# Rows of six experts exchanged by DMA, normalised on GpSimd and turned on VectorE instead of TensorE

## The reference

```python
x = x + layernorm(attn(layernorm(x)))   # gate g = sigmoid(x Wg^T + bg), scan h = (1-g) h + g x, out = h Wo^T + bo
x = x + layernorm(ffn(layernorm(x)))
# ffn: eid = argmax(softmax(xf @ router_w + router_b)); rank of the token among those of its expert
# valid = rank < C (320)
# expert: y = relu(buf[e] @ w1[e] + b1[e]) @ w2[e] + b2[e]     E = 8, D = 256, H = 1024, buf[e] is [320, 256]
# out = y of its expert where valid, otherwise relu(xf @ ow1 + ob1) @ ow2 + ob2
```

## Time and profile before

| | |
|---|---|
| median of 3 runs | 1139.37 us (1139.37 to 1139.41) |
| the profiled execution's own time | 1139.46 us |
| its span, first to last instruction | 1137.5 us |
| mean granted TensorE clock | 0.996 |
| PE, DVE, ACT, POOL busy share | 98%, 87%, 68%, 58% |
| steps of the experts | from about 990 us to the end |

### The profile page before, as it was taken

How to read it: one execution, slowest core, us unless ns; L and a number is a source line. 1 busy time by engine, 2 the same in 40 slices (tenths; PEclk the granted TensorE clock), 3 DMA queues, 4 the chain that set the end, 5 groups by cost and what they waited for, 6 DMA issues and landing times. The chain is left out here.

```text
span 1137.5 us, 24653 instructions
## 1 busy us (share of the span) xinstructions
PE 1118.9 (98%) x7341; PEld 996.5 (88%) x7341; DVE 989.5 (87%) x2795; ACT 772.7 (68%) x1433; POOL 661.6 (58%) x734
## 2 busy tenths in 40 slices
PE   8999999999999999999999999999999999999996
PEld 4788988888888898888888888898889988899996
DVE  6888899899999999998989898999999888688885
ACT  5366676667766667666677666677666776687882
POOL 3556666656666665666666666566666655324443
PEclk9999999999999999999999999999999999999998
DMA  8211043222222222222222222222222220435430
GB/s 259 68 48 57 20 126 80 72 76 56 74 74 74 74 74 73 69 72 70 72 53 72 73 57 72 60 71 74 74 74 74 55 93 20 128 126 175 159 126 31
DMA packets 186314, 92.46 MB, mean 81 GB/s; under 512 B 121403, under 2 KB 182509, under 8 KB 186148
## 3 DMA queue, kind: packets, MB, share of 16 engines
q1 hardware_dynamic: 179108, 86.65, 27.3%
q0 software_dynamic: 7168, 5.34, 1.6%
HBM read 53.82 MB, written 38.76 MB: 81 GB/s over the span
## 5 line engine op out<-in xcount | busy, mean ns | idle before, releaser
L691 ACT ACTIVATE hid<-psH,biasT 128x512 f32<-128x512 f32 (+1 forms) x312 | 202.7, 650 | 206.0 <-PE psH L1432 203.9
L1538 PE MATMUL psY<-W_hi,hid_hi 128*128 128x256 f32 x1168 | 336.1, 288 | 0.3 <-DVE hid_lo L1112 0.2
L1541 PE MATMUL psY<-W_hi,hid_lo 128*128 128x256 f32 x1168 | 330.5, 283 | 0.0
L1540 PE MATMUL psY<-W_lo,hid_hi 128*128 128x256 f32 x1168 | 330.3, 283 | 0.0
L1430 PE MATMUL psH<-xfT_hi,W_hi 128*128 128x512 f32 (+1 forms) x624 | 235.8, 378 | 0.3 <-ACT hid L691 0.2
L1112 DVE TENSOR_TENSOR hid_lo<-hid,hid_hi 128x512 fp32r<-128x512 f32 (+1 forms) x308 | 200.1, 661 | 40.3 <-ACT hid_hi L696 37.0
L1431 PE MATMUL psH<-xfT_lo,W_hi 128*128 128x512 f32 (+1 forms) x624 | 235.0, 377 | 0.0
L1432 PE MATMUL psH<-xfT_hi,W_lo 128*128 128x512 f32 (+1 forms) x624 | 232.6, 373 | 0.0
L1538 PEld LDWEIGHTS psY<-W_hi,hid_hi 128*128 128x128 f32 x1168 | 223.0, 191 | 9.2 <-issue 1.5
L1540 PEld LDWEIGHTS psY<-W_lo,hid_hi 128*128 128x128 f32 x1168 | 223.3, 191 | 6.0
L1541 PEld LDWEIGHTS psY<-W_hi,hid_lo 128*128 128x128 f32 x1168 | 223.1, 191 | 0.0
(11 more groups left out here) (179 smaller groups left out, 2167.5 us busy)
## 6 DMA issues: line engine op xcount, KB each, us to landing
xin<-L_attn_x SPq DMA_DIRECT2D x32, 512.0 KB, 3.5
stage<-L_ffn_w SPq DMA_DIRECT2D x16, 1024.0 KB, 5.5
out<-outt SPq DMA_DIRECT2D x31, 512.0 KB, 2.8
stage<-L_attn_x SPq DMA_DIRECT2D x26, 512.0 KB, 3.5
stage<-tok SPq DMA_DIRECT2D x416, 32.0 KB
xbuf<-zrow SPq DMA_DIRECT2D x1, 2590.0 KB, 16.8
xin<-xbuf SPq DMA_DIRECT2D x8, 259.0 KB, 5.3
stage<-L_ffn_ow SPq DMA_DIRECT2D x2, 1024.0 KB, 8.8
```

Source lines behind the costliest of these rows:

```text
L691: act.activation(hid[j % 2][:, at:n], psH[:, j % 2, at:n], ACT.Relu, bias=bias).then_inc(s_hid, 1)
L1538: pe.matmul(dst, hi, w[0][:, j, :], start=(j == 0 and (tail or t % 2 == 0)), stop=False, skip_group_check=True)
L1540: pe.matmul(dst, hi, w[1][:, j, :], start=False, stop=False, skip_group_check=True)
L1541: last = pe.matmul(dst, lo_, w[0][:, j, :], start=False, stop=(j == HC - 1), skip_group_check=True)
```

## The change

For experts 2 to 7 (`blocked`), the normalised and transposed rows come about in another way. SyncE loads the rows a second time from `xbuf` in DRAM, in twelve DMAs a step: for each quarter of the partitions, the 32x32 squares of each half of the features, exchanged so that a square's feature block selects the partitions and its token block the columns (`xblk`, in the buffer `keep`), and the two scalars of each token (`sblk`, in `ngx`). GpSimd multiplies and adds the scalars, two tensor_tensor for each, and VectorE turns each 32x32 square into `psT`. VectorE's `norm2` at j = 2 and TensorE's transposes go for these experts. The rows in `xe` are still loaded for the residual; GpSimd's copy of them waits for the load instead of for `tok2`.

```diff
+def blocked(e):
+    return not isinstance(e[0], int) or 2 <= 2 * e[0] + e[1] < E
...
+        xblk = keep[:].rearrange("p c n -> p (c n)")[:, 0:DC * C].rearrange("p (n c) -> p n c", c=C)
+        sblk = ngx[:, 0, 0:2 * (C // SQ)].rearrange("p (b k) -> p b k", k=2)
+        tok2_blk = tok2[:].rearrange("p t d -> p (t d)")[:, 0:DC * C].rearrange("p (n c) -> p n c", c=C)
...
+            def load_blocks(e):
+                i, v = e
+                rows = xbuf.rearrange("(e b r) w -> e r b w", r=SQ, b=C // SQ)[i * 2 + v]
+                if blocked(grp(i, v, -1)):
+                    sp.wait_ge(s_tok2, cnt(grp(i, v, -1), 1, 1) + NG)
+                sp.sem_inc(s_held_sp, 1)
+                sp.wait_ge(s_scan, 2 * NG)
+                for a in range(P // SQ):
+                    quad = slice(a * SQ, (a + 1) * SQ)
+                    sp.dma_start(sblk[quad], rows[:, :, D + 1:D + 3]).then_inc(s_xblk[v], 16)
+                    for n in range(DC):
+                        sp.dma_start(xblk[quad, n, :].rearrange("p (b c) -> p b c", c=SQ),
+                                     rows[:, :, n * P + a * SQ:n * P + (a + 1) * SQ]).then_inc(s_xblk[v], 16)
...
                 load_w1(far)
...
+                if blocked(far):
+                    load_blocks(far)
...
                 load_w2(far)
...
-                pool.wait_ge(s_tok2, cnt(e, 1, 1) + NG)
+                if blocked(e):
+                    pool.wait_ge(s_xe[v], landed(e, 2))
+                else:
+                    pool.wait_ge(s_tok2, cnt(e, 1, 1) + NG)
...
+            def norm_blocks(e):
+                i, v = e
+                pool.wait_ge(s_xblk[v], landed((i - 1, v), 3 * (P // SQ)))
+                pool.wait_ge(s_T1, cnt(e, 2, 0) + 2 * NG)
+                pool.sem_inc(s_held, 1)
+                for k, (src, op) in enumerate(((xblk, ALU.mult), (tok2_blk, ALU.add))):
+                    if k:
+                        pool.wait_ge(s_scaled, cnt(e, DC, -DC))
+                        pool.sem_inc(s_held, 1)
+                    for n in range(DC):
+                        last = pool.tensor_tensor(tok2_blk[:, n, :].rearrange("p (b c) -> p b c", c=SQ),
+                                                  src[:, n, :].rearrange("p (b c) -> p b c", c=SQ),
+                                                  sblk[:, :, k:k + 1].to_broadcast([P, C // SQ, SQ]), op)
+                        if k == 0:
+                            last.then_inc(s_scaled, 1)
+                last.then_inc(s_tok2, 1)
...
                     deviation(3, prev, ET, NG)
+                if live(nxt, E) and blocked(nxt):
+                    norm_blocks(nxt)
                 if live(prev, E):
                     rows_of(prev)
...
+            def turn_rows(e):
+                dve.wait_ge(s_tok2, cnt(e, 1, 1) + NG)
+                for c in range(DC):
+                    dve.transpose(psT[:, c, 0:C], tok2_blk[:, c, :]).then_inc(s_T1, 1)
...
-                        if j == 2:
+                        if j == 2 and not blocked(nxt):
                             norm2(nxt, xe, ET, NG)
+                        if j == 5 and blocked(nxt):
+                            turn_rows(nxt)
...
-                    if j == HC - 1 and live(nxt, E):
+                    if j == HC - 1 and live(nxt, E) and not blocked(nxt):
                         transposes1(nxt, ET, NG)
```

More of the change, by code:

```diff
@@ L276, in sandwich_kernel @@
         s_xe = sems("s_xe")
+        s_xblk = sems("s_xblk")
+        s_scaled = sem("s_scaled")
         s_oidx = sem("s_oidx")
```

## The result

The changed kernel takes 1145.11 us (median of 6 runs, 1145.05 to 1145.44) where the kernel before, beside it, takes 1139.43: a ratio of 1.0049, 95% interval 1.0039 to 1.0059. It is 5.7 us slower. The forecast was 9.0 us slower, 1148.5, with a range of 1141 to 1157.5. The profiled execution took 1145.22 us, span 1143.3.

A forecast was written before the change was run, and what follows sets the result against it. TensorE was taken to set the rate, with VectorE just in time. TensorE's -3.9 us and about +12.9 us for late VectorE net +9.0 on 1139.46: 1148.5 us, 8 in 10 between 1141 and 1157.5.

The forecast's parts named there:

- the saving: TensorE drops six transposes a step: -0.65 us a step, -3.9 us over six, if nothing else is late.
- the signs that the prediction named: Changed profile: steps of 17.9 to 18.5 us, W_lo at j = 3 and `lo` of chunk 4 over 1 us.
- GpSimd first: At chunk 4, GpSimd's second addition precedes `lo`, which ends at 11.85, 1.1 us late: +1.8 us a step.
- VectorE first: At chunk 4, `lo` precedes GpSimd's second addition, which ends at 13.7 with VectorE's transposes waiting: +1.3 us a step.
- The slack at chunk 4: Before layer 2 of chunk 4, `lo` ends at 10.73 and TensorE takes it at 10.89: 0.16 us.
- The cast: GpSimd's CAST of 128x3, 1.31 us in the trace, done at 12.75 with the COPY behind it.
- eats nearly all of the 0.65 us: VectorE's two transposes at j = 5, 0.82 us together, delay layer 2 of chunk 6 to 14.55.
- Rival 3: TensorE's 0.65 us a step comes back whole if `lo` of chunk 6 ends before 13.8: 1135.5 us, chance 0.05.
- Removing them brings nothing to chunk 4: VectorE's three tensor_scalar at j = 2, 1.05 us, stood before a hole; removal only lengthens it.
- The DMAs: Twelve more a step on SP's queue, 0.65 us each, 7.8 us; the next w2 load stays hidden.
- Rival 4: SP's queue issues take 1 us or more, w2 lands late: 1160 us, chance 0.09.
- Rival 5: GpSimd's four new instructions take 1.3 us each: +3 us a step, 1157 us, chance 0.08.

The follow-up runs named there:

- third run: Changed kernel with only GpSimd's COPY of the rows moved behind the three indirect stores: 1141.69 us, ratio 1.0021.
- fourth: Kernel before with TensorE's six transposes left out of the six steps, nothing in their place: 1138.82 us, ratio 0.9993.
- sixth: Kernel before with only GpSimd's COPY moved behind the three indirect stores: 1139.66 us, ratio 1.0001.
- second run: Changed kernel without GpSimd's four tensor_tensor and with the COPY behind the three indirect stores: 1139.64 us, ratio 1.0001.
- seventh: Changed kernel, GpSimd normalising at step start, twelve loads before w1's, VectorE turning at j = 3, COPY behind the stores: 1137.96 us, ratio 0.9981.
- eighth: The seventh kernel, but VectorE turns at j = 5 as in the changed kernel: 1141.27 us, ratio 1.0014.
- tenth run: The kernel of the ninth run, with ScalarE making the weights' fourth high eighth before the previous expert's layernorm: 1138.23 us, ratio 0.9986.
- ninth run: The seventh kernel with the COPY moved into the next step's hole, normalisation starting earlier: 1136.89 us, ratio 0.9976.
- first run: Changed kernel without GpSimd's four tensor_tensor, all DMAs, waits and VectorE transposes kept: 1143.24 us, ratio 1.0033.

## Why the prediction held, and what was off

**The direction and the mechanism were right.** TensorE was named as just fed by VectorE at chunks 4 and 5, and the three places where it waits now are chunk 4, chunk 5 and chunk 6, released by `lo`. GpSimd's and VectorE's turns at the port (the way into SBUF that the prediction has the two share) and VectorE's transposes at j = 5 both show, and the runs split them: the transposes take back the saving, the COPY costs 3.4 to 3.6 us, GpSimd's new work 1.9 to 2.4. Of the signs that the prediction named, two missed in size: the steps are 17.5 to 17.7 us long, not 17.9 to 18.5, and W_lo at j = 3 and `lo` of chunk 4 took 0.83 and 0.85 us, not over 1.

**The order came, its times were too long.** Of the two orders that I laid out for chunk 4, the first came (GpSimd first): first addition, W_lo, second addition, `lo` of chunk 4, each whole. "VectorE first" didn't come; the second addition ended at 10.70 of the step, not 13.7, and VectorE's transposes never waited for it. But the first path was forecast at +1.8 us a step and measured +0.94. In it `lo` of chunk 4 was to end at 11.85, and it ended at 11.05. That is the term that was mis-sized, and it adds up piece by piece: the multiplications were done at 8.65 and not 9.05 (0.90 and 0.73 us long, the first held up by `lo` of chunk 3); the first addition at 9.56 and not 10.05, since one alone takes 0.73 us and not 0.90; W_lo took 0.55 us behind it for 0.65, the second addition 0.59 behind W_lo for 0.80, `lo` 0.35 for 0.40. From there on the path held: `lo` of chunk 5 came 2.50 us later in both, `lo` of chunk 6 another 1.80 for 1.85. An instruction that has stood waiting for its turn needs 0.14 us less behind the other than it takes alone (0.49 and 0.35, 0.69 and 0.55, 0.73 and 0.59), and I had priced it nearly whole.

That the forecast, 9.0 us, lies nearer to 5.7 than the 10.8 of this path is luck: it was drawn down by the +1.3 of an order that didn't come.

The slack at chunk 4 was read as 0.16 us, "about the time a semaphore needs". Where TensorE waits for `lo` in the changed kernel, it starts 0.05 to 0.06 us after the recorded end of `lo` (1074.78 to 1074.84, 1077.28 to 1077.34, 1079.08 to 1079.13), so some 0.1 us was real slack: `lo` of chunk 4 is 0.32 us later and TensorE loses 0.25 in front of it.

**The cast.** I left it 1.3 us. It took 0.45. The COPY came at 12.17 of the step as soon as the residual was done, onto `lo` of chunk 5. The forecast had the COPY there in one of its two orders. That meeting costs 3.4 us of the changed kernel (third run). It was hidden before under the very transposes that were removed, as the fourth and sixth runs show: neither alone brings a microsecond.

**The transposes on VectorE.** Forecast 0.41 us each of VectorE's time: 496 ns is the median recorded, and W_lo starts 0.82 us after the first of the two, 0.41 each. Forecast "eats nearly all of the 0.65 us"; the second run measured 1139.64 against 1139.58, and its six steps took 99.5 us against 99.9, so 3.5 to 3.9 of the 3.9 us. Rival 3 (faster) needed `lo` of chunk 6 before 13.8; it ended at 15.35, and at 14.3 even in the second run.

**The hole.** "Removing them brings nothing to chunk 4" held. What I didn't follow up is that the hole is where the new transposes belong: 2.8 to 3.3 us (seventh and eighth runs).

**The DMAs.** SP issued the twelve in 6.3 us in one step and 7.8 in the step before it, against 7.8 forecast, and the next w2 was issued at 1081.61, 17.9 of the step. ScalarE never waited for it. Rival 4 didn't come. Rival 5 (1.3 us an instruction) didn't either.

SP's row of the profiled kernel, all 48 loads of squares (duration ns min/median/max), and GpSimd's:

```profile
L422 SPq DMA_DIRECT2D keep<-xbuf x48: 318/366/1437, 1007.0 to 1098.5; - x48
```

```profile
L644 POOL TENSOR_TENSOR tok<-keep,ngx x12: 728/808/977, 1017.8 to 1106.7; 128x320 f32<-128x320 f32 x12
L644 POOL TENSOR_TENSOR tok<-tok,ngx x12: 733/958/1184, 1019.6 to 1108.3; 128x320 f32<-128x320 f32 x12
```

GpSimd's least, 728 ns, is what one costs alone; the longest, 1184, has a VectorE instruction in front of it.

**What stays open.** Who gets the port when both ask is not settled. In the changed kernel the two engines alternate, one whole instruction each, even where GpSimd's two additions follow without a wait. But in the tenth run W_lo waited through two multiplications, and before, GpSimd's CAST of 128x3 waited through W_lo and `lo` of chunk 3 together: it ended 0.05 us after `lo`. Nor does the recorded start decide: W_lo kept its turn in the ninth run where it started 0.20 us ahead of the multiplication (1010.41), and lost it in the tenth at 0.42 to 0.45. GpSimd's recorded starts are rough.

## What to carry to other kernels

A saving on the engine that sets the rate is worth only what the next engine's order lets through: look at every place where work of the bound engine covers a late producer, and remove the lateness in the same edit (here the transposes covered a COPY that cost 3.4 us without them). New work on a second engine belongs in a hole that the timeline shows, not where the code before had its counterpart; moving the same two transposes from j = 5 to j = 3 brought 2.8 to 3.3 us. GpSimd work over SBUF is best laid beside VectorE's idle time or, as the COPY of the ninth run (0.83 us for 1.04), beside its transposes, which read one tensor.

## What was unexpected of the hardware

- A VectorE tensor_tensor of 128x512 with two SBUF inputs took 2.42 to 2.46 us, for 0.68, in five steps of the tenth run, when two GpSimd tensor_tensor without a wait between them began 0.42 to 0.45 us after its recorded start. It got its turn in the first gap of GpSimd's (0.18 us) and ended 0.55 to 0.57 us after the second of them.
- A GpSimd CAST of 128x3 took 0.19 us with VectorE idle (first run), 0.35 in the ninth, 0.45 in the changed kernel and 1.31 in the kernel before. In the last three it ended 0.05 us after a `lo` of VectorE's.
- Where a GpSimd and a two-input VectorE instruction meet, the one that waits ends a fixed time after the other: `lo` 0.34 to 0.35 us, W_lo 0.54 to 0.55, an addition or multiplication of 128x320 0.59 to 0.60, the COPY 0.69 to 0.70, the CAST 0.05, in all six steps of the changed kernel.
- Each wait of TensorE costs about 0.10 us beyond itself (0.07 to 0.11): the second matmul behind it also starts late (0.22 between starts for 0.12).
